# Blocks' y rows transposed by DMA, block 3's bias split on GpSimd, first expert list read sooner, three scatter-adds of one expert in flight

## What is computed

```python
x = x + xattn(layernorm(x), ctx)          # 2048 rows of 256, in 4 batches of 512 rows
x = x + moe(layernorm(x))

def xattn(y, Z, ...):                     # y: (4, 512, 256), Z: 1601 rows of context
    y = layernorm(y + attention(y, y, y, causal=True), g1, beta1)
    y = layernorm(y + attention(y, Z, Z, causal=False), g2, beta2)
    h = relu(y @ w1 + b1)                 # 256 -> 1024
    return layernorm(y + h @ w2 + b2, g3, beta3)

def moe(x, wg, w1, w3, w2):               # 8 experts, top 2 of the softmax, weights made to sum to 1
    y_e = (silu(x @ w1[e].T) * (x @ w3[e].T)) @ w2[e].T
    return sum over a row's two experts of weight * y_e
```

## Time and profile before

| | us |
|---|---|
| median of 3 runs | 558.45 (558.25 to 559.0) |
| profiled execution | 560.24 |
| its span, first to last instruction | 557.8 |
| PE busy | 503.5 (90%) |
| DVE busy | 383.5 (69%) |
| POOL busy | 294.7 (53%) |
| ACT busy | 291.2 (52%) |

### The profile page before, as it was taken

One profiled execution on the slowest core, in us unless ns is written; L12 is line 12 of the kernel. 1 busy time (PEld: TensorE's weight loads), 2 busy tenths in 40 slices (PEclk: granted clock), 3 DMA queues, 4 the chain that ended last, 5 costly groups with the idle time before them and its releaser, 6 DMA issues. The chain is left out here.

```text
span 557.8 us, 11154 instructions
## 1 busy us (share of the span) xinstructions
PE 503.5 (90%) x3753; PEld 333.2 (60%) x3753; DVE 383.5 (69%) x977; ACT 291.2 (52%) x592; POOL 294.7 (53%) x331
## 2 busy tenths in 40 slices
PE   4999999979899998899999977779999899999981
PEld 2676766745566675577565666545566556666651
DVE  5799886688877577867876789988767534344440
ACT  2647867574747546673558373564554333443420
POOL 3564030016423519826795629473667565667564
PEclk9999999999999999999999999999999999999995
DMA  8021615238878257832765543125795688787763
GB/s 273 2 71 25 198 58 152 77 71 160 155 170 141 86 73 145 175 90 77 147 142 135 162 101 125 39 76 105 122 182 97 114 113 124 131 127 132 132 86 38
DMA packets 131090, 64.57 MB, mean 116 GB/s; under 512 B 105533, under 2 KB 122366, under 8 KB 131038
## 3 DMA queue, kind: packets, MB, share of 16 engines
q1 hardware_dynamic: 123550, 53.64, 44.2%
q0 software_dynamic: 7488, 10.23, 11.5%
HBM read 28.19 MB, written 10.35 MB: 69 GB/s over the span
## 5 line engine op out<-in xcount | busy, mean ns | idle before, releaser
L1132 PE MATMUL ps<-arena,probT 128*128 128x256 f16 (+2 forms) x1092 | 181.8, 320 | 7.0 <-DMA probT<-prob 4.4
L1132 PEld LDWEIGHTS ps<-arena,probT 128*128 128x128 f16 (+1 forms) x1092 | 105.8, 98 | 65.5 <-issue 10.3
L901 POOL DMA_INDIRECT out<-y,qst x39 | 62.5, 1604 | 28.3 <-issue 13.9
L946 ACT ACTIVATE prob<-ps,nbias 128x512 f16<-128x512 f32 x64 | 39.0, 610 | 71.5 <-DVE nbias L1647 71.5
L1132 PE MATMUL ps<-arena,qT 128*128 128x512 f16 (+1 forms) x384 | 70.8, 337 | 5.4 <-DVE prob L1782 5.3
L2181 DVE SCALAR_TENSOR_TENSOR ps<-ps,w1m 128x512 f32<-128x512 f32 x39 | 27.4, 703 | 54.6 <-ACT w1m L1075 54.5
L1075 ACT ACTIVATE w1m<-ps 128x512 f32<-128x512 f32 x39 | 23.3, 597 | 75.5 <-PE ps L1132 75.5
L1132 PE MATMUL ps<-arena,tT 128*128 x468 | 58.2, 276 | 2.8 <-DVE tT L2277 2.8
L1132 PEld LDWEIGHTS ps<-arena,qT 128*128 128x128 f16 x384 | 33.0, 98 | 41.2 <-issue 8.4
L1132 PE MATMUL ps<-tT 128*128 128x512 f16 (+3 forms) x240 | 52.7, 360 | 2.1 <-DVE tT L1609 2.1
L1132 PE MATMUL ps<-w2s,tT 128*128 128x256 f16 x384 | 48.4, 273 | 5.7 <-DVE tT L1850 5.6
(11 more groups left out here) (216 smaller groups left out, 983.0 us busy)
## 6 DMA issues: line engine op xcount, KB each, us to landing
stage<-we_in SPq DMA_DIRECT2D x33, 256.0 KB, 2.9
prob<-we_in SPq DMA_DIRECT2D x15, 256.0 KB, 2.9
xin<-x_in SPq DMA_DIRECT2D x16, 128.0 KB, 2.8
out<-y SPq DMA_DIRECT2D x16, 128.0 KB
hrow<-tT SPq DMA_DIRECT2D x4, 512.0 KB, 3.1
y<-x_in SPq DMA_DIRECT2D x3, 512.0 KB, 6.4
stage<-z_in SPq DMA_DIRECT2D x4, 256.0 KB, 5.2
prob<-w_in SPq DMA_DIRECT2D x4, 256.0 KB, 2.9
```

Source lines behind the costliest of these rows:

```text
L901: g.indirect_dma_start(out[:rows_of(p), :], bass.IndirectOffsetOnAxis(ridx[:, n:n + 1], 0), ys[:, n % RING, :], None, compute_op=ALU.add). ...
L946: a.activation(row_cols(q, 0, c), ps[c][:, :w], ACT.Exp, bias=nbias[:, q, :], scale=SM)
L1132: r = t.matmul(o, lhs(a), rhs(b), start=first and n == 0, stop=last and n == 2)
```

## The change

1. **y rows cross by DMA.** For the twelve tiles of blocks 0 to 2 and the first two tiles of block 3, ACT copies a row tile of y to float16 (`y_row_hi`), DVE subtracts (`y_row_lo`), both into a free half of `nrm` (tiles 12 and 13: of `stage`), and SP issues two DMA transposes (`y_turn`). PE's transposes, ACT's `y_hi` and DVE's `y_lo` stay for unit 4 alone. The copies stand at the ends of the steps: row i-1 in step i, for i of 1 to 13; where a feed-forward unit runs, inside it.
2. **SP's order in a step.** All three turns come first, then the loads; the loads of x stand earlier by a place.
3. **POOL** waits, ahead of each normalisation of tile i of 2 to 13, for the transposes of row i-2, whose source it overwrites. Block 3's b2 is added in two halves, the first, with `x_beta(3)`, behind unit 2's.
4. **DVE.** The self-attention's last normalisation goes behind the low parts of step 0; the first expert list is read at chunk 2 of unit 4 instead of 4; `table_rest(0)` goes behind `y_lo`; at the end the copy for the last tile goes ahead of one weighted tile.
5. **Scatter-adds.** Four semaphores instead of two, and an add waits for the one three before it; for the two between only if the expert changed (for n-2 also at every n with n % 4 == 1, and in the first tiles).

```diff
@@ SP
             for i in range(NT - 1):
+                if i - 1 in FIRST and i < NT - 2:
+                    y_turn(i - 2)
                 if i + 3 < NT:
                     q_turn(i + 3)
-                turn(i + 1, 0)
+                for p in range(len(TURNS)):
+                    turn(i + 1, p)
                 loads(step_from(i), step_from(i) + STEP_PIECES[i])
-                turn(i + 1, 1)
-                turn(i + 1, 2)
...
+                if 0 < i < NT - 3 and i not in FIRST:
+                    y_turn(i - 1)
+            def y_turn(n):
+                wait(sp, "y_rlo", n + 1)
...
+                for a in range(2):
+                    sp.dma_start_transpose(y_turned(n, a), y_row(n)[:, a * D:(a + 1) * D]
+                                           ).then_inc(sm[f"y_t{n % 2}"], 16)
@@ ACT, c_step
                 split_step(split_hi, act_, i + 1)
+                if 0 < i < NT - 2:
+                    y_row_hi(i - 1)
+            def y_row_hi(n):
+                wait(act_, "c_y", n + 1)
...
+                copy(y_row(n)[:, :D], y[:, n, :]).then_inc(sm["y_rhi"], 1)
@@ DVE, c_step
-                if i == 0:
-                    s_norm(NB - 1)
                 split_step(split_lo, dve, i)
...
                 between(early[1:], own)
+                if i == 0:
+                    s_norm(NB - 1)
                 sums("c_", 1 - q, C_CH, i + 1, C_CH * (i + 2))
                 if i + 4 < NT:
                     q_lo(i + 4)
...
+                if 0 < i < NT - 2:
+                    y_row_lo(i - 1)
                 for f in late:
                     f()
+            def y_row_lo(n):
+                wait(dve, "y_rhi", n + 1)
+                v.tensor_tensor(y_row(n)[:, D:], y[:, n, :], y_row(n)[:, :D], ALU.subtract).then_inc(sm["y_rlo"], 1)
@@ DVE, step 15
             hid_lo(3, 5)
-            table_rest(0)
             hid_lo(3, 6)
...
-            y_lo(4)
+            y_lo()
+            table_rest(0)
...
-                if f == 4:
+                if f == 2:
                     list_read(0)
-                if f == 2:
                     for m in range(TB):
                         x1_stats(2, m)
@@ DVE, end
-            weighted(NJ - 2, (NJ - 2) % RING)
             wait(dve, "e_ltr", 2)
             v.tensor_copy(actT[:, (NJ - 1) % RING, 1].rearrange("p k c -> p (k c)"),
                           last_bank(1)).then_inc(sm["e_lcp"], 1)
+            weighted(NJ - 2, (NJ - 2) % RING)
@@ POOL
             def ln_affine(pre, i, q, row):
                 pool.wait_ge(sm[pre + "rstd"], i + 1)
+                if 2 <= i < 3 * TB + 2:
+                    pool.wait_ge(sm[f"y_t{q}"], 32 * (i // 2))
...
+                    if j == 2:
+                        x_beta(NB - 1)
+                        y_b2_last(0)
             out_ends(2)
-            y_b2(NB - 1)
+            y_b2_last(1)
...
             gather(1)
-            x_beta(NB - 1)
@@ POOL, add(n)
+                alone = n <= RING or n == PHASES[p][1]
+                if n > 2:
+                    add_done(n - 3)
+                if n > 1 and (alone or n % RING == 1):
+                    add_done(n - 2)
+                if n and alone:
+                    add_done(n - 1)
+                if not alone:
...
-                    pool.wait_ge(sm[f"e_add{1 - n % 2}"], done)
+                    pool.wait_ge(sm[f"e_add{(n - 1) % RING}"], done)
+                    if n % RING != 1:
+                        pool.wait_ge(sm[f"e_add{(n - 2) % RING}"], done)
@@ PE
             def up(u, f):
-                if f == 0:
-                    wait(pe, "f_ylo", KD * (u + 1))
+                if f == 0 and u < 4:
+                    for q in range(2):
+                        wait(pe, f"y_t{q}", 32 * ((UNITS[u][0] * TB + UNITS[u][2]) // 2))
...
                 u = AFTER[i]
-                y_trans(u, i)
                 c_pv(i)
```

129 lines of the change are left out of this document (73 added, 56 removed).

## The result

The changed kernel takes **577 to 578 us**: a median of 578.2 (574.3 to 583.5) in the first comparison and 577.1 (573.4 to 582.3) in a second, against 558.5 and 558.0 for the kernel before. The ratio is 1.033, with intervals of 1.026 to 1.040 and 1.030 to 1.037. The ratios leave out as slow the single executions that lie over 1.5% above the fastest of their kernel (583.5 and 582.3 of the changed kernel, one each of the kernel before, e4 and e10); without them the changed kernel's medians are 576.2 and 577.0. Slower was forecast, with 570.0 and a range to 575: the sign is right, the size is not, and the median lies above the range.

What follows compares the result with a forecast made beforehand. DVE's row of work, not only PE, was taken to pace the cross-attention steps, and PE the expert loop. Terms of +16.5, -1.5, -2 and -1.5 summed to +11.5 us: a median of 570.0 us, range 561.5 to 575.

Steps and rivals of the forecast that it cites:

- half microsecond for the late rows of y: Units 1 and 2: the last y row crosses behind x1's store, half a microsecond after the first up now starts.
- term 2: Other y rows, steps 5 to 14: transposes and waits saved against added work; -1.5 us, bounds -5 and +4.
- reordering priced at nothing: Last units: DVE's table work moves behind y_lo, taken as a mere reordering without cost.
- term 3: Last feed-forward units and first expert list: DVE's bound stretch gets shorter; -2 us, bounds 0 and -4.
- carrying over of one profiled execution's distance from its median: Whole kernel: the profiled execution stood 1.8 us above the median, so 571.7 profiled became a median of 570.0.
- term 1: Cross-attention steps 1 to 4: copy, subtraction and maxima of y wait for late loads; +16.5 us, bounds +13 and +23.5.
- term 4: Scatter-adds at the end: three under way let the last ones go sooner; -1.5 us, bounds 0 and -2.
- The fast case: Rival, steps 1 to 4: loads are in place when ACT comes to its splits, no coupling; 549 us, 7%.
- The 1.3 us at step 0: Step 0: tile 2's exponentials come about 1.3 us sooner, half of PE's 2.57 us wait for the lows.
- The claim that three edits must meet: Steps 1 to 4: the coupling comes from late loads, copy behind the splits and subtraction ahead of the maxima together.
- The -3.5 of the prediction's other reading: Last units: if DVE and GpSimd lock their port pair exclusively, all 2.6 us come back, about -3.5 us.
- SP binds as well: Rival, six plain steps: SP's 8.8 us list delays turns or loads land late; +5 more, 575 us, 15%.

Runs made afterwards that it cites:

- e4: The kernel before with only the scatter-add and tail-copy edits: 557.1 us, ratio 0.998.
- e10: As e9, with table_rest(0) back in its old place: 556.1 us, ratio 0.995.
- e6: The kernel before with only its expert loads moved behind all three turns (DMA transposes): 567.1 us, ratio 1.014.
- e5: The changed kernel with DVE's subtraction of y moved behind the four maxima and the bias: 579.7 us, ratio 1.039.
- e14: The changed kernel with y's two turns ahead of the x loads and x1 stores of their step: 575.9 us, ratio 1.033.
- e13: As e10, with y's two turns ahead of the x loads and x1 stores of their step: 551.6 us, ratio 0.991.
- e15: As e13, with at most two scatter-adds under way: 554.9 us, ratio 0.996.
- e3: The changed kernel with ACT's copy of y ahead of its splits and the loads behind the first turn: 559.8 us, ratio 1.006.
- e12: The changed kernel with table_rest(0) back in its old place: 576.3 us, ratio 1.033.
- e9: As e3, with ACT instead of SP issuing the expert loads in steps without feed-forward: 556.3 us, ratio 0.995.

## Why the prediction was right and wrong

The mechanism that makes the kernel slower was the forecast one. The steps that failed are the half microsecond for the late rows of y and the gains beside it (term 2), the reordering priced at nothing (term 3), and the carrying over of one profiled execution's distance from its median; term 1 was sized too low by 2.0 us. In the first profile term 4 erred by 3.4 us the other way and hid half of what the other three missed.

- **Term 1 (+16.5): right in mechanism and place, 2.0 short**, within its bounds. Of the 15.45 us of step 2, lows and third turn took 6.6 (6.4 summed), the second load's later issue 0.8 (0.5), its landing 4.3 (3.7), its split 0.6 (0.6), copy to exponentials 3.1 (3.2). So it was the loads that were mis-sized: the two took 2.26 us to issue, for the 1.06 that I read from the kernel before, and landed later. In step 3 the chain went through the first load's landing and both splits and came out as summed, 14.5. Step 4 took 14.2 for 13.4; the 13.4 holds a half microsecond that none of my terms gives, since by the count of step 1 it is 13.9. Unit 0's first ups behind the last gap ran slow as told: 5.5 us to the first down product for 3.9. The fast case hung on ACT's wait for the stages ending early; it lasted 4.5 to 6.3 us.
- **The 1.3 us at step 0** came as a number by luck: tile 2 starts at 130.78 for 131.85, but also at 130.78 in e4, which lacks that edit. The edit did take PE's wait away (0.28 us for 2.57). What I left out is that it also moves GpSimd's part of the self-attention's last normalisation 2.4 us later, and beside it DVE's subtraction for q, which stands ahead of the next maxima, takes 2.53 us. In e4 it starts 0.6 us later, takes 1.90 and ends at the same time; in most other steps it takes 0.41:

```profile
125.91 2.53 DVE L1744 TENSOR_TENSOR stage<-y,stage 128x256 f16<-128x256 f32 x1
125.81 2.35 POOL L783 TENSOR_TENSOR y<-y,vec 128x1024 f32<-128x1024 f32 x1 [3.91 <-DVE y L1798]
```

- **The claim that three edits must meet** was too strong. The loads' place alone makes a good part of it (e6, +7.5 us), since the next exponentials stand behind the splits in ACT's list; my own numbers, without copy and maxima, give 11.2 us a step, more than 8.76. And "DVE ahead of the maxima" is no condition (e5).
- **Term 2 (-1.5): the wrong sign**, +2.4 and +0.5 in the two profiles. The step that failed is "by the same count half a microsecond": unit 2's last row waited 2.57 and 2.24 us, unit 1's 1.02 and 1.05. I counted x1's stores ahead of the turns and not the three loads of x that the change had put there. DVE was done at 308.1, the turns were issued at 310.19:

```profile
307.52 1.62 SPq L581 DMA_DIRECT2D xin<-x_in  x3
309.19 0.91 SPq L565 DMA_DIRECT2D out<-y  x2
310.19 1.17 SPq L630 DMA_TRANSPOSE probT<-nrm  x1
```

  That is not all of it. With the turns first (e14) the stretch still takes 149.9 us for 150.0, so the gain of 1.5 did not come either. PE's waits on line 1850 and 1844 (2.1 and 1.5 us) did go, but those for the low parts of the probabilities rose from 1.5 to 4.2 us (5.7 in e14), and those for turns, 1.8 before, stayed at 1.6. Nor does -1.5 follow from the items listed for it, which add to about -5 (transposes -2.25, waits -1.8, -2.1 and -1.5, DVE's row +2.4).
- **Term 3 (-2): -1.2** in the first profile and +0.5 in the second. "A reordering", priced at nothing, was not: it moved DVE's normalisation under GpSimd's multiplications and additions. I looked at the collision that the change took away and not for one it made. The first did go: no split of that stretch takes over 0.90 us in the changed kernel, for 3.32. In the seven profiles that have this part of the change and a short normalisation the stretch takes 41.0 to 41.9 us, 1.0 to 1.9 less than before; in the seven with a long one it takes 43.4 to 44.8. The -3.5 of the prediction's other reading came in none.
- **Term 4 (-1.5): -4.9** in the first profile and -1.9 in the second, expert loop and tail together. With an otherwise equal program the third add is worth 3.4 us (e13, e15), more than twice the term. That its error of -3.4 us in the first profile stands against term 2's of +3.9 is luck.
- **From one profiled execution to the median: 5.7 us of the 8.2 by the first profile, 1.9 of 7.1 by the second.** I carried over that the profiled execution stood 1.8 us *above* its median. The changed kernel's first stands 3.9 *below*, its second and e14's 0.1 below. By the second profile the terms are 5.9 us short in the span: 1.8 (term 1), 2.0, 2.5 and -0.4. One execution can't tell which of the two it is. Single executions of the changed kernel spread from 573.4 to 580.2 us, and those of the kernel before, timed often enough, from 554.1 to 561.5; the three runs shown (0.75 us apart) had hidden that. Executions with a lower mean clock are the longer ones (0.976 at 574.3 us, 0.966 at 580.2), but which comes first was not tried: neither PE's gaps (e3) nor the collision (e12) proved to be the cause, and this stays open.
- **The rivals.** "SP binds as well" did not happen in the changed kernel, where SP idled 4 us a step. It was true of the kernel without the coupling (e3). The fast case, 549 with the coupling gone, came near in e13 (551.6), but only once SP was relieved, the turns of y went first and the tables stood in their old place.

## What to carry to other kernels

When an engine takes its list in order, look at what is queued *behind* each wait on a transfer, on every engine: loads issued 3.1 us later cost 7.5 us by themselves, and with one more copy behind them, and what waits for that copy, the whole change lost 18 to 20. Opening such a ring at one link may show a second of the same length (e5), or the queue that fed it (e3), so price the bound behind the bound before counting the gain. And an edit that only reorders small vector work can put a wide instruction beside GpSimd's: check both engines at the new place, and don't take one profile's word for it: the same rows gave 0.74 us once and 4.83 once.

## What was not expected of the hardware

- Issuing a DMA transpose holds SP's queue about 1.2 us almost whatever its size: 1.17 us for 128x2x128 (y), 1.22 for 128x4x128 (q), 1.26 for 128x8x128, while a plain load of 128x512 float32 takes 0.53. Two half-size turns for a row of y therefore cost two full ones.
- Plain loads hold the queue for less when no turn goes ahead of them: 0.33 us on SP at 86 to 94 us, and 0.33 to 0.38 on ACT's queue (e9). Two of them behind three turns took from 1.18 to 2.26 us in the changed kernel.
- A 0.43 us DVE instruction took 4.83 to 5.58 us beside eight GpSimd instructions of 0.7 us in a row and did not get in between them; in e14, started at the same place, it took 0.74.
